# A four-step cross-attention loop whose steps' tails are interleaved with the next step's opening

## The reference

```python
x = layernorm(x + L0_attn(x))                 # its gates and norm: the "head" of a step
q, k, v = x @ wq.T + bq, ctx @ wk.T + bk, ctx @ wv.T + bv      # 16 heads of 8
s = where(mask, einsum('bhqd,bhkd->bhqk', q, k) / sqrt(8), -1e9)
o = einsum('bhqk,bhkd->bhqd', softmax(s), v)
x = layernorm(x + o @ wo.T + bo)
logits = x @ router_w.T                       # top 2 of 8, rank among the tokens of an expert
buf[expert, rank] += x                        # if rank < 641
```

## Time and profile before

| what | value |
| --- | --- |
| median of 3 runs (lowest, highest) | 993.28 us (990.33, 1000.54) |
| profiled execution: time, span | 990.89 us, 989.2 us |
| mean granted TensorE clock | 0.859 |
| busy PE, PEld, DVE | 725.4, 466.5, 535.5 us |
| busy ACT, POOL | 384.3, 161.8 us |
| DMA queues of the kind instruction, q8 and q14 | 24 and 32 packets, 0.39 and 0.26 MB |
| phase B: first `scores_q` to first row of the experts on PE | 297.9 to 605.5 us |

### The profile page before, as it was taken

One profiled execution on the slowest core, in us unless ns is written; L12 is line 12 of the kernel. 1 busy time (PEld: TensorE's weight loads), 2 busy tenths in 40 slices (PEclk: granted clock), 3 DMA queues, 4 the chain that ended last, 5 costly groups with the idle time before them and its releaser, 6 DMA issues.

```text
span 989.2 us, 13689 instructions
## 1 busy us (share of the span) xinstructions
PE 725.4 (73%) x4459; PEld 466.5 (47%) x4459; DVE 535.5 (54%) x1947; ACT 384.3 (39%) x892; POOL 161.8 (16%) x206
## 2 busy tenths in 40 slices
PE   5788696877739968977977944999257668666765
PEld 3445353443214654653654733888135436344442
DVE  3445264554337936936938630111245885877865
ACT  3624445263114633533541532323024354353533
POOL 9300000000201014014013013000421411311010
PEclk9897998998668988998995976999688789788887
DMA  7600000100221072063051001321110200200000
GB/s 213 189 11 11 1 22 0 28 26 0 59 52 55 7 90 65 0 86 74 0 70 32 2 6 56 84 57 50 40 43 1 54 11 2 54 12 12 0 12 11
DMA packets 49242, 39.47 MB, mean 40 GB/s; under 512 B 11233, under 2 KB 42657, under 8 KB 49186
## 3 DMA queue, kind: packets, MB, share of 16 engines
q1 hardware_dynamic: 47138, 34.62, 15.7%
q0 software_dynamic: 2048, 4.20, 1.6%
HBM read 27.20 MB, written 11.60 MB: 39 GB/s over the span
## 4 chain that ended last, share of the span: by engine, by line
PE 52%; DVE 25%; ACT 8%; issue 7%; DMA 4%; SPq 2%; POOL 1%; DVEq 0%; ACTq 0%; POOLq 0%
PE bank L1243 4%; PE bank L1232 4%; PE bank L1345 4%; DVE R L2177 4%; DMA q_stack<-parts_dram 3%; PE bank L1126 2%; PE bank L1129 2%; PE bank L1128 2%; PE bank L1139 2%; PE bank L986 2%; PE bank L918 2%; PE bank L1046 2%; PE bank L1098 2%; DVE bank L1895 2%; PE bank L1053 2%
## 5 line engine op out<-in xcount | busy, mean ns | idle before, releaser
L1895 DVE CUSTOM_DVE_ANT_0 bank<-bank,add_q 128x256 f32<-128x256 f32 x256 | 100.2, 456 | 30.3 <-PE bank L1098 18.0
L1558 ACT ACTIVATE pT<-bank 128x512 f32<-128x512 f32 x128 | 76.1, 597 | 72.9 <-PE bank L1129 70.6
L1345 PE MATMUL bank<-XT,kpad 128*128 128x256 f32 (+1 forms) x256 | 60.7, 368 | 16.1 <-DVE cT L2119 16.1
L1098 PE MATMUL bank<-k_stack,q_stack 96*128 96x256 bf16 x256 | 52.4, 303 | 26.9 <-DMA q_stack<-parts_dram 20.1
L1126 PE MATMUL bank<-q_stack,k_stack 96*128 96x256 bf16 x256 | 70.5, 275 | 1.9 <-DVE mx L1895 1.9
L1128 PE MATMUL bank<-add_k,ident_b 128*128 128x256 bf16 x256 | 70.8, 277 | 0.0
L1129 PE MATMUL bank<-neg_max,head_sel 96*128 96x256 bf16 x256 | 70.6, 276 | 0.0
L1345 PEld LDWEIGHTS bank<-XT,kpad 128*128 128x128 f32 x256 | 49.7, 216 | 26.4 <-DVE cT L2119 18.1
L2119 DVE TENSOR_TENSOR cT<-bank,decay 128x384 f32<-128x384 f32 x64 | 35.1, 554 | 48.3 <-POOL decay L868 28.9
L1583 ACT ACTIVATE he<-bank 128x324 f32<-128x324 f32 x64 | 28.2, 440 | 69.7 <-PE bank L1232 64.2
L868 POOL TENSOR_SCALAR_AFFINE_SELECT decay<-decay 128x256 f32<-128x256 f32 x64 | 26.8, 419 | 159.9 <-ACT decay L1652 159.9
(11 more groups left out here) (408 smaller groups left out, 1643.7 us busy)
## 6 DMA issues: line engine op xcount, KB each, us to landing
k_stack<-parts_dram SPq DMA_DIRECT2D x48, 64.0 KB
q_stack<-parts_dram SPq DMA_DIRECT2D x24, 128.0 KB, 7.8
expert_in<-no_rows SPq DMA_DIRECT2D x8, 324.0 KB, 4.1
rows<-expert_in SPq DMA_DIRECT2D x8, 324.0 KB
expert_out<-rows_y SPq DMA_DIRECT2D x8, 324.0 KB
moe_w<-in_L_ffn_w_dram SPq DMA_DIRECT2D x1, 2048.0 KB
parts_dram<-k_parts SPq DMA_DIRECT2D x4, 384.0 KB, 2.5
parts_dram<-q_parts SPq DMA_DIRECT2D x12, 128.0 KB, 1.7
```

The costliest lines, as they stand in the source:

```text
L1098: last = pe.matmul(q_bank(n)[:, c * S:(c + 1) * S], q_stack[:, h // 2, b * S + c * P:b * S + (c + 1) * P], k_stack[:, h // 2, h % 2, b * S ...
L1345: last = pe.matmul(c_bank(n)[:, lo:lo + width], kpad2[:, h, b * S + c * P:b * S + (c + 1) * P], XT[:, par, q0:q0 + width], start=True, sto ...
L1558: act.activation(pT[:, g % 2, j], k_bank(n)[:].rearrange("p (c q) -> p c q", c=QC), ACT.Exp).then_inc(exp_ready.sem, 1)
L1895: last = dve.tensor_tensor_reduce(sc, sc, add_q[:, b * QC + c, :], 1.0, 2.0 * NEG, ALU.add, ALU.max, mx[:, c, h:h + 1])
```

## The change

A tail is cut in functions, and each engine runs them inside the next step's opening and units. PE runs `joint(i)` in place of the opening of steps 1 to 3, and three parts of the tail go behind units 2, 4 and 6. DVE and ACT put the pieces behind numbered units. Only step 3's own tail (`end`) still stands alone. Stacks and masks are loaded and waited for by sequence (b = 0, b = 1): the half for b = 0 is loaded once the first 16 `scores_k` of the step are done. `ctxT` and `x_res` exist twice and are loaded a step ahead. `wo` and the tail's transposes use banks 0 and 3, `values_of` bank 2. All loops of phase B are written out.

SP:

```diff
-            def stack_q(i):
+                        sp.dma_start(k_stack[lo:lo + DH1, :, s, cols], of_heads(0, part)[DH1 * s:DH1 * (s + 1), :, cols]).then_inc(k_stacked[b].sem, 16)
+            def stack_q(i, b):
+                cols = slice(b * S, (b + 1) * S)
                 for j in range(3):
                     sp.wait_ge(*q_saved[j].at(i))
                     for r in [r for r, term in enumerate(TERMS) if term[0] == j]:
-                        sp.dma_start(q_stack[2 * DH1 * r:2 * DH1 * (r + 1)], of_heads(1, j)).then_inc(q_stacked.sem, 16)
+                        sp.dma_start(q_stack[2 * DH1 * r:2 * DH1 * (r + 1), :, cols], of_heads(1, j)[:, :, cols]).then_inc(q_stacked[b].sem, 16)
...
             load_ctxT(0)
             load_x(0)
             sp.wait_ge(*updated.at(0))
             load_masks(0)
             save_k(0)
-            stack_k(0)
+            load_ctxT(1)
+            for b in range(NB):
+                stack_k(0, b)
+            sp.wait_ge(*x_in_used.at(0))
+            load_x(1)
             save_q(0)
-            stack_q(0)
-            def mix(i, following):
-                if following:
+            for b in range(NB):
+                stack_q(0, b)
+            def mix(i):
+                wait_apart(sp, passed, *masks_ready.at(i))
+                load_masks(i + 1)
+                for b in range(NB):
+                    sp.wait_ge(*k_stacked[b].at(i))
+                save_k(i + 1)
+                if i + 2 < STEPS:
                     sp.wait_ge(*v_aug_ready.at(i))
-                    load_ctxT(i + 1)
-                    sp.wait_ge(*x_in_used.at(i))
-                    load_x(i + 1)
-                    wait_apart(sp, passed, *masks_ready.at(i))
-                    load_masks(i + 1)
-                    save_k(i + 1)
-                    save_q(i + 1)
-                    sp.wait_ge(*sT_ready.at(i))
-                    stack_k(i + 1)
-                    stack_q(i + 1)
-            with sp.Fori(0, STEPS - 1) as i:
-                mix(i, True)
+                    load_ctxT(i + 2)
+                sp.wait_ge(*sT_ready.at(i, H1))
+                stack_k(i + 1, 0)
+                if i + 2 < STEPS:
+                    sp.wait_ge(*x_in_used.at(i + 1))
+                    load_x(i + 2)
+                for b in range(NB):
+                    sp.wait_ge(*q_stacked[b].at(i))
+                save_q(i + 1)
+                stack_q(i + 1, 0)
+                sp.wait_ge(*sT_ready.at(i))
+                stack_k(i + 1, 1)
+                stack_q(i + 1, 1)
+            for i in range(STEPS - 1):
+                mix(i)
```

POOL:

```diff
+            for i in range(STEPS):
+                following = i + 1 < STEPS
+                if following:
+                    split_k(i + 1)
+                if i > 0:
+                    send_rows(i - 1)
+                if following:
+                    wait_apart(pool, passed, *sT_ready.at(i, H1))
+                    masks(i + 1, 0)
+                    residual(i + 1)
+                    wait_apart(pool, passed, *sT_ready.at(i))
+                    masks(i + 1, 1)
+            send_rows(STEPS - 1)
```

PE, opening and units:

```diff
+            def joint(i, following):
+                t = i - 1
+                scores_q(i, 0)
+                values(t, 1, G - 1)
+                scores_q(i, 1)
+                if following:
+                    keys(i + 1)
+                scores_q(i, 2)
+                scores_q(i, 3)
+                outputs_T(t, 1)
+                scores_q(i, 4)
+                if following:
+                    head(i + 1, 0)
+                tokens_T(t)
+                scores_q(i, 5)
+                if following:
+                    head(i + 1, 1)
+                project(t)
+                scores_q(i, 6)
+                values_of(i)
+                scores_q(i, 7)
+                if following:
+                    head(i + 1, 2)
+                scores_q(i, 8)
+                scores_q(i, 9)
+                maxima_T(i, 0)
+                scores_q(i, 10)
+                if following:
+                    head(i + 1, 3)
+                for n in range(11, AHEAD):
+                    scores_q(i, n)
+                if following:
+                    head(i + 1, 4)
+                    head(i + 1, 5)
...
+                        if i > 0 and n == 2:
+                            rows_T(i - 1)
+                        if i > 0 and n == 4:
+                            route(i - 1)
+                        if i > 0 and n == 6:
+                            count_ranks(i - 1)
+                        if n > 0 and (n + AHEAD - 2) % 8 == 0 and n + AHEAD - 2 < XU + 1:
+                            maxima_T(i, (n + AHEAD - 2) // 8 - 1)
```

ACT:

```diff
+            def joint(i, following):
+                t = i - 1
+                copy_outputs(t, 1, 1)
                 if following:
                     keys(i + 1)
-                    for n in range(5):
+                    head(i + 1, 0)
+                turn_outputs(t)
+                if following:
+                    for n in range(1, 5):
                         head(i + 1, n)
+                    act.preload_act_table_set(LOG_EXP)
+                roots(mv_m, log_var_m, recip_m, var_m, rstd_m, lambda s, n: s.at(t, n))
```

DVE:

```diff
+            def heads(i, following, tail_chain):
+                t = i - 1
+                chain = Chain(dve, dve_m, i)
+                head_chain = Chain(dve, dve_h, i + 1) if following else None
+                for n in range(XU):
+                    score(i, n)
+                    if n % 8 == 1 and n > 8:
+                        negated(i, n // 8 - 1, chain)
+                    if following and n in later:
+                        head(i + 1, later[n], head_chain)
+                    if i > 0:
+                        if n == 1:
+                            normalise(t, 1, tail_chain)
+                        if n == 5:
+                            add_residual(t, tail_chain)
+                        if n == 6:
+                            values(i)
+                        if n == 13:
+                            norm_rows(t)
+                        if n == 16:
+                            pick_experts(t, tail_chain)
+                        if n == 19:
+                            place_rows(t, tail_chain)
+                        if n == 21:
+                            gates_of(t, tail_chain)
+                negated(i, MG - 1, chain)
+                if following:
+                    head(i + 1, 9, head_chain)
+                normalise(i, 0, chain)
```

More of the change, by code:

```diff
@@ L1209, in mix, with begin @@
                 last.then_inc(ranks.sem, 1)
+            def begin():
+                for n in range(AHEAD):
+                    scores_q(0, n)
+                    if n == 9:
+                        maxima_T(0, 0)
+                    if n == 0:
+                        keys(1)
+                    elif n in (2, 4, 6, 8, 10, 12):
+                        head(1, n // 2 - 1)
+            def joint(i, following):
[32 more added lines that the diff above has]
+                    head(i + 1, 5)
@@ new lines, in _, with heads @@
+            later = {4: 6, 9: 7, 17: 8, 20: 9}
+            def heads(i, following):
+                for g in range(NB * G):
+                    for n in range(4 * g, 4 * g + 4):
+                        scores_k(i, n)
+                        ahead = n + AHEAD
+                        if ahead < XU:
+                            scores_q(i, ahead)
+                        if i > 0 and n == 2:
[7 more added lines that the diff above has]
+                        if following and n in later:
+                            head(i + 1, later[n])
+                    if g == 6:
+                        outputs_T(i, 0)
+                    if g > 0:
+                        values(i, (g - 1) // G, (g - 1) % G)
@@ L1211, in experts, with end @@
+            def end(t):
+                values(t, 1, G - 1)
+                outputs_T(t, 1)
+                tokens_T(t)
+                project(t)
+                rows_T(t)
+                route(t)
+                count_ranks(t)
             def experts():
@@ L1419, in _ @@
             values_of(0)
-            with pe.Fori(0, STEPS - 1) as i:
-                mix(i, True)
-            mix(STEPS - 1, False)
+            for i in range(STEPS):
+                if i == 0:
+                    begin()
+                else:
+                    joint(i, i + 1 < STEPS)
+                heads(i, i + 1 < STEPS)
+            end(STEPS - 1)
             experts()
@@ L1687, in _ @@
                 head(0, n)
-            with act.Fori(0, STEPS - 1) as i:
-                mix(i, True)
-            mix(STEPS - 1, False)
+            for i in range(STEPS):
+                if i == 0:
+                    keys(1)
+                    for n in range(5):
+                        head(1, n)
+                else:
+                    joint(i, i + 1 < STEPS)
+                heads(i, i + 1 < STEPS)
+            end(STEPS - 1)
             experts()
```

(16 more changed lines are left out.)

370 lines of the change are left out of this document (176 added, 194 removed).

## The result

The changed kernel takes 985.2 us (median of 20 runs, 980.96 to 990.99), the kernel before 992.1 in the same comparison (20 runs, 984.93 to 1000.54): ratio 0.993, 95% interval 0.991 to 0.995. It is faster, by 7 us and not by the 30 of the forecast: the interval excludes 1, but 0.7% is less than the 1% within which the prediction called a result the same. 985.2 lies near the upper end of the range. The profiled execution spans 984.2 us, 5.0 less than before; where the 30 went is the question.

A forecast was written before the change was run, and what follows sets the result against it. PE's 58.7 us of gaps, waiting for stack loads with the tail's path nearly as long, were the bound. Gaps -55.7 and longer steps summed to -35.4, taken as -30: 961 us profiled, 963 median, range 946 to 986.

The forecast's parts named there:

- T0: The prediction's mark for a step's first `scores_q` on PE, from which it timed the step.
- L: The prediction's mark for a step's last `scores_k` on PE, where the gap to the next step begins.
- the gaps: PE between a step's last `scores_k` and the next first `scores_q`: 58.7 us in all, of which 55.7 go.
- q half: Load of the b = 0 half of the q stack: taken to land in 3.5 us, just in time by 0.2 to 2.
- The hand schedule: Steps 1 to 3, tail's hand-offs meeting as computed: steps grow by 7.4, 7.4 and 6.6 us; whole sum -35.4.
- the uncertain 0.4 of later `maxima_T`: Steps 1 and 2: added for late `maxima_T`, raising each step's growth from 7.0 to 7.4 us.
- the allowance of 5.4 for missed hand-offs: Steps 1 to 3: one unit (0.8 us) missed at two of six hand-offs each costs 5; -35.4 becomes -30.
- B: Step starts: b = 0 halves land 8.3 to 9 us late at three places, +26, 989 us; chance 0.09.
- A: Tail hand-offs in the steps wait as today, some 2 us each, 6.5 a step: 977 us; 0.21 with E.
- D: Steps: added work falls into idle time, 59 to 60 us a step against 64, 947 us; chance 0.13.
- C: DVE or PE at step starts: instruction supply stalls, 6.03 us each, seven make it slower, 1005 us; chance 0.07.
- E: Starts of steps 1 and 2: DVE's loop gap stays, +11, 974 us; lies inside A, 0.21 together.

The follow-up runs named there:

- paced: Changed kernel with a step's eight indirect DMAs spread out, one after every second `scores_k` from the eighth on: 964.1 us, ratio 0.972 to the kernel before.
- the fourth kernel: Kernel before with POOL's part written out and each step's scatter held until the next step's sixth `scores_k`: 1009.1 us against 991.9, ratio 1.018.

## Why the prediction was wrong

The terms of its sum, measured from T0 and L of each profile (L as the start of the `values` behind the last `scores_k`), in us against the kernel before:

| term | forecast | changed | paced |
|---|---|---|---|
| the gaps | -55.7 | -55.7 | -55.7 |
| step 1, L - T0 | +7.4 | +17.3 | +10.7 |
| step 2 | +7.4 | +16.2 | +11.7 |
| step 3 | +6.6 | +18.7 | +11.4 |
| up to the first L | -1.5 | -3.6 | -3.5 |
| behind the last L | +0.4 | +2.2 | 0.0 |
| sum (span) | -35.4 | -5.0 | -25.4 |

Each number is rounded by itself. The terms before the first L and behind the last L hold work that the change doesn't touch, and single executions differ there by more than the terms: the loops written out alone show -6.6 and +3.0, the kernel without the DMAs -2.0 and +3.4. Only the gaps and the three steps bear a reading to 0.1 us.

**The step that failed** is a half sentence: "POOL splits keys before it scatters, and scatters with 15 us to spare before masks are wanted." It costs the moved DMAs by POOL's own queue and by who waits for POOL, and asks nothing of what runs beside them. They cost 18.3 us in the three steps (changed less paced, and changed less the kernel without them); the fourth kernel lost as much in the old order, 18.7 in its steps and 17 of its time. The rows of before could not have given the price, but they could have given a bound. Beside the DMAs the old kernel's windows are (steps 1, 2 and 3):

```profile
373.50:389.00 15.50, 13.99 (x43) 5.60 (x44) 9.90 (x48) 7.21 (x9) 10.51 (x11) 0.82 0.25 84
449.20:464.70 15.50, 13.68 (x43) 5.54 (x44) 9.90 (x48) 7.22 (x9) 9.99 (x11) 0.84 0.25 85
523.00:535.00 12.00, 7.81 (x30) 3.06 (x30) 11.35 (x58) 0.00 (x0) 7.79 (x8) 0.50 0.11 42
```

43 matmuls in 15.5 us, 30 in 12.0, partly or wholly at half clock: 2.5 to 2.8 a microsecond, where the changed kernel runs 7.7 (77 in 10.0, above). No row of before has the two together, so "nothing" had no row under it, and the cost belonged among the rivals.

**The gap**: right, to 0.1 us, and for its reason. The q half landed 2.2 us after its issue (1.9 to 2.8), not 3.5. That both the loads and the tail must move is half tested: with the loads late and the tail moved nothing is gained.

**The hand schedule**: right up to unit 14, which DVE starts 21.1 us after T0 as computed (PE 0.6 before it). The row at 391.23 that the prediction takes for this unit is the one before it, and unit 14 is the row at 392.12; the sum doesn't hang on it. DVE's first unit stands 0.6 us after T0. DVE waits 1.1 us for `outputs_T` (1.7 forecast) and 1.4, in step 3 2.2, for the router (1.9). Behind that it was too short. In the paced kernel unit 31 ends 52.4, 53.4 and 46.7 us after T0 (50.0, 50.0, 42.6), and from there to L it is 13.9, 13.9 and 12.6 (12.5 and 11.9). The term that was mis-sized is "the uncertain 0.4 of later `maxima_T`"; DVE's waits in the paced kernel's step 1 have it:

```profile
DVE neg_max L2020 <- PE bank L1141: 3.3, 2, 2.7
...
DVE logits L2062 <- PE bank L1216: 1.4, 1, 1.4
```

3.3 in step 1 and 3.9 in step 2, where before has 0.5; in step 3 it is 1.2, and 2.3 more for which the profile names no releaser. The kernel without the DMAs has the same 3.3, 3.9 and 3.5, so they are no part of it. PE comes late to `maxima_T(2)`, since it had waited for the tail and then ran at a granted clock of 0.83 (380 to 390 us; 0.66 in step 2, 448 to 458), with the DMAs and without. The clock was forecast at 1.00 for the openings only, and there it was (steps 1 and 2). These misses make 12.4 us over three steps; the allowance of 5.4 for missed hand-offs covered less than half.

**The rivals.** 985.2 lies at the foot of B's interval (984 to 995), but B's mechanism isn't there: no q half is late. A (977) says what was left of the loss, in another form: late hand-offs, 12 us where it had 19.5. (Six hand-offs at 2 us, less 4.2, are 7.8 a step and not 6.5, which makes A 981; and D's 947 starts from the profiled 990.9, where the others start from the median, by which it is 949.) C isn't there: no wait of 6 us for issue. E isn't either: the loop gap goes, and is worth nothing. D (947) needed DVE never to wait, and it waited. The loss of 18 to 20 us had no rival at all. That the result still fell inside the range is luck: the gap's gain and this loss met in it.

The paced kernel shows the forecast's own order free of it: span -25.4 against -30, time 964.1 against 963.

## What to carry to other kernels

When work is moved, ask of each instruction not only what it waits for and who waits for it but what ran beside it in the old place and what will in the new; a cost of nothing that was read beside an idle or half-clock engine does not hold beside a full one. When all engines stand still at once and the profile names no releaser among them, look at what the one busy engine is doing, and move that alone. A burst of indirect DMAs from POOL beside dense matmuls is cheap to spread: one for two units of PE's work cost nothing here. And test the parts of a large change apart: here the early loads carried 28 us once the tail had moved, the written-out loops gave nothing that can be told, and the new place of the indirect DMAs lost 18 to 20.

## What the runs showed of the hardware

POOL's indirect DMAs hold back TensorE. Eight of them, issued some 1.3 us apart, cost 1.2 to 4.9 us to 180 bf16 matmuls with neither waits nor readers (once 10.5, most of it at half clock), 4 to 10 us to stretches whose results ACT or DVE read (`values`, in fp32 on 32 columns, the most), and nothing to `scores_q` alone at 2.6 matmuls a microsecond, to fp32 matmuls on 128 columns alone, or at the 1.2 GHz level; plain DMAs of POOL and SP of the same size and tensor operations of POOL cost nothing. Among other work fp32 matmuls are not safe: the 5.5 us at `values_of` (fp32, 128 columns) came in an opening with 45 matmuls in 7.0 us. The DMAs themselves are not slowed: the last packet of step 1's last one was done 1.9 us after its issue, as in the kernel before. The records don't always show it at PE: there a matmul's start may be in its place while the results come up to 6.7 us later (`values` of step 3, 535.02 against 541.69), and the only sign is an engine that waits with no releaser named. The Trainium skill, SBUF — State Buffer, section SBUF: two separate sides, says that on the engines' side only the port pair that VectorE and GpSimd share is contended for, and that "PE, ACT, and DVE's dedicated pair never wait on anyone." If the hold is in the SBUF, the measurement speaks against that: PE alone took 23.8 us for 20.1 us of matmuls beside POOL's eight indirect DMAs. Through what POOL holds PE is not shown by any run here.
